# Two clips of the expert layer moved: two relus on ScalarE, and a product that subtracts on VectorE

## What is computed

```python
g = jnp.minimum(p1[..., 0::2], LIMIT)             # LIMIT = 7
lin = jnp.clip(p1[..., 1::2], -LIMIT, LIMIT)
act = g * jax.nn.sigmoid(ALPHA * g) * (lin + 1.0)
p2 = jnp.einsum('bsei,ehi->bseh', act, mlp2_weight) + mlp2_bias
combined = jnp.einsum('bseh,bse->bsh', p2, combine)   # combine: two weights of eight are not zero
```

## Time and profile before

| | |
|---|---|
| median of 3 runs | 915.94 us (915.14 to 916.11) |
| the profiled execution's own time | 917.65 us |
| its span, first to last instruction | 915.9 us |
| mean granted TensorE clock | 0.976 of full speed |
| busy: PE, DVE, ACT, POOL | 841.9, 712.3, 721.0, 484.2 us |

### The profile page before, as it was taken

One profiled execution on the slowest core, in us unless ns is written; L12 is line 12 of the kernel. 1 busy time (PEld: TensorE's weight loads), 2 busy tenths in 40 slices (PEclk: granted clock), 3 DMA queues, 4 the chain that ended last, 5 costly groups with the idle time before them and its releaser, 6 DMA issues.

```text
span 915.9 us, 37757 instructions
## 1 busy us (share of the span) xinstructions
PE 841.9 (92%) x15768; PEld 547.1 (60%) x15768; DVE 712.3 (78%) x1785; ACT 721.0 (79%) x1251; POOL 484.2 (53%) x786
## 2 busy tenths in 40 slices
PE   4569999999999999999999999999999999998996
PEld 2335666657566665756666575666657566665645
DVE  7666868879787887978788797878879787786635
ACT  4337888888788888888788888888888888877785
POOL 6417446382735638283653827366382736445352
PEclk9758999999999999999999999999999999999999
DMA  5952417133351613334261323416133341610101
GB/s 127 227 88 84 75 43 142 56 104 44 119 80 56 142 55 103 44 125 75 66 130 56 104 43 123 76 61 136 55 100 47 113 76 50 135 44 7 31 2 36
DMA packets 85597, 75.14 MB, mean 82 GB/s; under 512 B 9457, under 2 KB 79154, under 8 KB 85426
## 3 DMA queue, kind: packets, MB, share of 16 engines
q1 hardware_dynamic: 83346, 71.93, 34.9%
q10 hardware_dynamic: 2080, 0.79, 0.4%
HBM read 36.26 MB, written 30.15 MB: 73 GB/s over the span
## 4 chain that ended last, share of the span: by engine, by line
PE 64%; DVE 14%; issue 10%; ACT 7%; POOL 2%; DMA 2%; SPq 1%; POOLq 0%; DVEq 0%; ACTq 0%
PE ps L571 11%; PE ps L513 8%; PE ps L843 6%; PE ps L805 6%; PE ps L502 5%; PE ps L794 3%; PE ps L590 2%; DVE mx L1221 2%; PE ps L528 2%; PE ps L811 2%; PE ps L585 2%; ACT h L1077 2%; PE ps L719 2%; PE ps L781 2%; DVE act_t L1368 2%
## 5 line engine op out<-in xcount | busy, mean ns | idle before, releaser
L1221 DVE TENSOR_REDUCE mx<-ps 128x2 f32<-128x320 f32 (+1 forms) x512 | 219.7, 466 | 101.9 <-PE ps L528 100.8
L1004 ACT ACTIVATE pt<-ps 128x1024 f32<-128x1024 f32 (+1 forms) x256 | 232.9, 914 | 39.5 <-PE ps L502 37.2
L1487 POOL TENSOR_SCALAR_AFFINE_SELECT pt<-pt 128x512 f32<-128x512 f32 x256 | 162.3, 637 | 140.5 <-ACT pt L1004 139.5
L513 PE MATMUL ps<-kd,qz 48*32 48x160 bf16 (+1 forms) x4096 | 146.1, 236 | 13.8 <-issue 6.7
L502 PE MATMUL ps<-qz,kd 51*32 51x256 bf16 (+1 forms) x4096 | 153.6, 261 | 0.8 <-issue 0.7
L794 PEld LDWEIGHTS ps<-m,act_t 128*128 128x128 f32 x1024 | 128.1, 191 | 39.6 <-DVE act_t L1368 23.6
L571 PE MATMUL ps<-pt,va 128*32 128x256 f32 (+1 forms) x2048 | 145.2, 364 | 2.1 <-POOL pt L1490 0.9
L794 PE MATMUL ps<-m,act_t 128*128 128x128 f32 x1024 | 140.0, 280 | 7.6 <-DVE act_t L1368 5.7
L513 PEld LDWEIGHTS ps<-kd,qz 48*32 48x32 bf16 x4096 | 77.9, 92 | 105.9 <-issue 52.3
L1490 POOL TENSOR_SCALAR_AFFINE_SELECT pt<-pt 128x512 f32<-128x512 f32 x192 | 122.1, 636 | 0.0
L1037 ACT ACTIVATE lin<-ps,mbias 128x512 f32<-128x512 f32 x128 | 87.5, 684 | 35.5 <-DVE act_t L1368 22.9
(11 more groups left out here) (187 smaller groups left out, 1560.1 us busy)
## 6 DMA issues: line engine op xcount, KB each, us to landing
qz<-qk_parts SPq DMA_DIRECT2D x32, 384.0 KB, 6.4
kd<-qk_parts SPq DMA_DIRECT2D x32, 384.0 KB, 10.0
qk_parts<-qp SPq DMA_DIRECT2D x16, 384.0 KB, 3.1
qk_parts<-kp SPq DMA_DIRECT2D x16, 384.0 KB, 2.8
xl<-L_attn_x SPq DMA_DIRECT2D x16, 256.0 KB, 3.5
qk_parts<-qp SPq DMA_DIRECT2D x16, 256.0 KB, 3.1
qk_parts<-kp SPq DMA_DIRECT2D x16, 256.0 KB, 2.9
xnr<-xn SPq DMA_DIRECT2D x16, 256.0 KB, 2.5
```

What stands on the lines that cost most here:

```text
L513: nc.tensor.matmul(ps[QG * c:QG * (c + 1), 4 + par, w * pr:w * (pr + 1)], qz[q][rows, 2 * g + pr, P * i + QG * c:P * i + QG * (c + 1)], kd ...
L1004: nc.scalar.activation(to, src, ACT.Exp, scale=SCALE).then_inc(exp_ok.sem, 1)
L1221: nc.vector.tensor_reduce(mx[:, i, HG * g + pr:HG * (g + 1):2], src, AX.X, ALU.max).then_inc(mx_ok.sem, 1)
L1487: sel1 = nc.gpsimd.affine_select(out=pt[:, s, :, 0:P], in_=pt[:, s, :, 0:P], compare_op=ALU.is_ge, fill=0.0, base=0, pattern=[[0, HG], [1, ...
```

## The change

For the experts 4 and 6 (`TWICE`) the clip is made by two relus on ScalarE. The first takes the place of the plain eviction, with a bias of b + 1 + (LIMIT - 1), and gives max(p1, -7) + 7. The second (`clip_high`) reads and writes `lin` in SBUF, with a scale of -1 and a bias of 2 LIMIT, and gives 7 minus the clipped value; it stands right behind `evict_gate(e)` in ACT's list. VectorE has no clip for these two, and their product subtracts 1 + LIMIT from `lin` before it multiplies, which gives the product with its sign turned. The mask `sel` holds -1 in place of 1 for them, so that `gc` is negative too. For this the masks are made in 24 instructions (8 experts, 3 parts) in place of 3.

```diff
+TWICE = (4, 6)
+SIGNS = tuple((e, -1.0 if e in TWICE else 1.0) for e in range(8))
...
+        span = sb("span", [P, 1])
...
-            (half[:], -0.5), (ident[:], 0.0), ...
+            (half[:], -0.5), (span[:], 2.0 * LIMIT), (ident[:], 0.0), ...
...
                 def evict_lin(e):
                     act.wait_ge(*done(up_ps, b, e + 1))
                     act.wait_ge(*(done(act_ok, b, e - 1) if e >= 2 else done(act_ok, b - 1)))
-                    nc.scalar.activation(lin[:, e % 2], bank(3 * (e % 2) + 1), ACT.Identity, bias=mbias[:, e, 1:2]).then_inc(lin_ok.sem, 1)
+                    if e in TWICE:
+                        nc.scalar.activation(lin[:, e % 2], bank(3 * (e % 2) + 1), ACT.Relu, bias=mbias[:, e, 1:2]).then_inc(low_ok.sem, 1)
+                    else:
+                        nc.scalar.activation(lin[:, e % 2], bank(3 * (e % 2) + 1), ACT.Identity, bias=mbias[:, e, 1:2]).then_inc(lin_ok.sem, 1)
+
+                def clip_high(e):
+                    act.wait_ge(*done(low_ok, b, TWICE.index(e) + 1))
+                    nc.scalar.activation(lin[:, e % 2], lin[:, e % 2], ACT.Relu, scale=-1.0, bias=span[:]).then_inc(lin_ok.sem, 1)
...
                             evict_gate(e)
+                            if e in TWICE:
+                                clip_high(e)
...
+                dve.wait_ge(consts.sem, 3)
+                for e in TWICE:
+                    nc.vector.tensor_scalar(mbias[:, e, 1:2], mb_b[:, e, 1:2], 1.0, LIMIT - 1.0, ALU.add, ALU.add).then_inc(consts.sem, 1)
...
                 def clip(e):
 
+                    if e in TWICE:
+                        return
...
-                        dve.wait_ge(*done(clip_ok, b, e + 1))
-                        nc.vector.tensor_tensor(act_t[:, e % 3], lin[:, e % 2], gc[:, e % 2], ALU.mult).then_inc(act_ok.sem, 1)
+                        if e in TWICE:
+                            dve.wait_ge(*done(lin_ok, b, e + 1))
+                            nc.vector.scalar_tensor_tensor(out=act_t[:, e % 3], in0=lin[:, e % 2], scalar=1.0 + LIMIT, in1=gc[:, e % 2],
+                                                           op0=ALU.subtract, op1=ALU.mult).then_inc(act_ok.sem, 1)
+                        else:
+                            dve.wait_ge(*done(clip_ok, b, e + 1 - sum(t < e for t in TWICE)))
+                            nc.vector.tensor_tensor(act_t[:, e % 3], lin[:, e % 2], gc[:, e % 2], ALU.mult).then_inc(act_ok.sem, 1)
...
-                        pool.wait_ge(masks_set.sem, 7 + c)
-                    nc.gpsimd.affine_select(out=sel[:], in_=sel[:], compare_op=ALU.not_equal, fill=1.0, base=-E * c, pattern=[[-1, E], [0, P]],
-                                            channel_multiplier=1).then_inc(masks_set.sem, 1)
+                        pool.wait_ge(masks_set.sem, 7 + E * c)
+                    for e, sign in SIGNS:
+                        nc.gpsimd.affine_select(out=sel[:, e], in_=sel[:, e], compare_op=ALU.not_equal, fill=sign, base=-E * c - e, pattern=[[0, P]],
+                                                channel_multiplier=1).then_inc(masks_set.sem, 1)
```

More of the change, by code:

```diff
@@ L60 @@
 TIE = -1e-37
-CONSTS = 4
+CONSTS = 6
 AT_STATES, AT_H0, AT_Q, AT_K, AT_U, AT_V, AT_G, AT_C = 2, 3, 4, 6, 8, 10, 12, 14
@@ L309, in build @@
         lin_ok = signal("lin_ok", E)
-        clip_ok = signal("clip_ok", E)
+        low_ok = signal("low_ok", len(TWICE))
+        clip_ok = signal("clip_ok", E - len(TWICE))
         gc_ok = signal("gc_ok", E)
@@ L371, in build @@
         BLANKS = [
-            (half[:], -0.5), (ident[:], 0.0), (identb[:], 0.0), (bw[:, N:], 0.0), (cw[N:, :], 0.0), (ncw[:], 0.0), (b2st[:], 0.0),
+            (half[:], -0.5), (span[:], 2.0 * LIMIT), (ident[:], 0.0), (identb[:], 0.0), (bw[:, N:], 0.0), (cw[N:, :], 0.0), (ncw[:], 0.0), (b2st[:], 0.0),
             (edge[:], 0.0), (first[:], 0.0), (tie[:], 0.0), (sel[:], 0.0), (bias3[:], 0.0), (onesb[:], 1.0),
@@ L383, in build @@
         ALL_BLANKS = len(BLANKS) + len(LATER_BLANKS)
-        N_MASKS = 7 + NPART
+        N_MASKS = 7 + NPART * E
         qk_d = nc.dram_tensor("qk_parts", (2, P, 6, T), BF16, kind="Internal").ap()
```

## The result

The changed kernel takes 927.35 us (median of 4 runs, 925.24 to 927.63) against 915.92 (4 runs, 915.14 to 916.11): a ratio of 1.0109, 95% interval 1.0092 to 1.0126. The medians lie 11.4 us apart, the ratio gives 10.0 us (8.4 to 11.5). It is slower, as forecast, and inside the range, near its upper end; forecast were 8.4 us more, at 924.4. The profiled execution took 927.32 us, where 926.1 had been forecast for it.

The account below looks back on a forecast made before the run. ACT's full list was taken to hold h2T, for which PE's MLP waits. 15 x 0.55 + 0.18 = 8.4 us took the profiled 917.65 to 926.1, the median to 924.4; range 921.0 to 928.0.

Parts of the forecast that it names:

- Second relu of expert 4: On ACT between ga 4 and lin 5: hidden in the idle time before lin 5, with 0.2 us to spare.
- Second relu of expert 6: On ACT between ga 6 and lin 7, no idle time: delays h2T by 0.55 us a pass, ends 0.48 and 0.67.
- Pass 0: lin 7 there follows 0.26 us of idle time, so the delay is 0.18 us, with ends at 0.11 and 0.30.
- What waits behind h2T: PE's MLP follows 0.55 us later, its wait grows from 0.47 to 1.0 us; no second stall, nothing given back.
- First relu: On ACT in place of an Identity eviction from PSUM of the same tile: zero difference, at the dearest 0.10 us more.
- Clips of 4 and 6: Removed from DVE: product 4 comes 0.36 us earlier, product 6 does not move; gain on the path 0 for both.
- The product with a subtraction: On DVE, in place of the plain product of 0.69 us: no difference taken.
- Prologue: 24 mask selects on POOL take at most 7.0 us, covered by its wait for DVE: cost 0, without cover 3.4 once.
- A hidden delay: Rival: PE waits for something else behind L805 for at least 0.45 us a pass, time stays near 916; chance 0.08.
- A part given back in the attention stage: Case in which part of the delay is given back in the attention stage; chance 0.03.
- Relief of DVE: Rival: one clip of 0.36 us comes off each pass, 5.8 us in all, giving 910.1; chance 0.07.
- Table loads: Rival: relu needs another ACT table, 1.28 us a load, 61 us and 8.4, some 985; chance 0.02.

Follow-up runs that it names:

- The relu that nobody reads: Kernel before, all clips on VectorE, plus an unread relu behind ga 6 on ACT: 930.07 us against 916.26, the second time 927.35 against 916.45.
- the swap: h2T put ahead of lin 7 in ACT's list: 909.69 us against 916.45 in the kernel before; with relus for experts 2 and 3, 898.75.
- Expert 4 alone: The change made for expert 4 only, against the kernel before: 917.72 us against 917.32, ratio 1.0009.

## Why the prediction was right, point by point

- *h2T is held by ACT's own list, and a pass has no slack behind it.* Right. The relu that nobody reads delays `h2T` and the kernel with it; the swap makes both faster.
- *Second relu of expert 4: hidden.* Right. It starts 0.57 after ga 4, as worked out. Between its start and that of lin 5 are 0.77 us, of which it needs 0.61 to 0.62: 0.15 to spare, not 0.2, as the same price was set too low. Expert 4 alone costs nothing that can be measured.
- *Second relu of expert 6: on the path.* Right in place, too small in size. This is the mis-sized term: 0.55 us a pass was taken, 0.62 measured. I had placed it under the eviction of 0.69 us for its SBUF source; it takes 0.72, more than that eviction. The overlap with the next instruction was taken at 0.12 and is 0.11. Over 15 passes this made the forecast 1.0 us too low.
- *Pass 0.* `h2T` 12.86 us after `aoT` before and 13.08 after: 0.22 for 0.18.
- *What waits behind h2T.* Right that nothing gives the delay back: the shortest stretch to the next `aoT` is 40.50 us for 40.52. PE's wait was to be 1.0 us and is 1.22: product 5 comes 0.34 us earlier too, which had been left out, and lets down 5 end 0.13 earlier. That lengthens the wait and moves nothing.
- *First relu at no difference.* Right: L1042 takes 0.67 to 0.69, the eviction of before 0.67 to 0.70.
- *Clips of 4 and 6: no gain.* Right, the clip of 4 moves the products 4 and 5 by some 0.35 us and `h2T` not at all; product 6 stays in place, and so do the products of experts 2 and 3, whose moving was named as a sign of being wrong.
- *The product with a subtraction: no difference.* Right, 0.69, but for the one of pass 0.
- *Prologue: 0.* The masks took 6.34 us, within the bound of 7.0, and alone cost nothing measurable. The wait by which they are covered is 7.27 us.
- *The sum.* With the measured price it is 15 x 0.615 + 0.22 = 9.4 us, which the split of the span shows (9.40). The ratio gave 10.0 us at first and 10.4 us in a second comparison (927.43 against 916.26, ratio 1.0114, 1.0093 to 1.0135), the medians 11.4 and 11.2:

> The changed kernel once more, against the kernel before on one chip in five rounds. The stretch from the first aoT to h2T grew by 0.61 us in each of 15 passes and by 0.22 in pass 0: if nothing else is in the difference, the median ratio gives 9.4 us (9 to 10); if the prologue or another part costs as well, 11 us or more, as the first runs gave (11.4).

Both intervals hold 9.4 us (8.4 to 11.5, and 8.5 to 12.4). What the 0.6 to 2 us beyond 9.4 are is not settled. The profiled executions do not show them: 927.32 is 9.67 over 917.65, and outside `aoT` to `h2T` their spans come to 716.1 us before and to 716.2 and 716.0 changed. They may be chance: the median of the kernel before moved between 915.92, 917.32, 916.26 and 916.45 from set to set, and the kernel with the dead relu by 2.7 us. The part of the span outside `aoT` to `h2T` differs by 3 us between the two executions of the dead relu. That the change lengthens PE's pauses was neither shown nor shut out.

The forecast of 924.4 also took over that the profiled execution of before lay 1.71 us above its median. That of the changed kernel lies at its median. So of the 3.0 us between 924.4 and 927.35 the relu's price makes 1.0, and most of the rest is where the profiled executions happened to lie. The range was wide enough for both.

- *The rivals.* A hidden delay: no, PE shows no other wait. A part given back in the attention stage: no, by the shortest stretch. Relief of DVE: not at 4 and 6, but true at 2 and 3, ahead of product 3, where it is worth 0.34 us a clip. Table loads: none were added, 49 in both profiles. By the Trainium skill, "ScalarE: Activation LUTs", section Table sets, relu is in every set; the trace now agrees for Relu beside the sigmoid form of gelu. The rule of that page of the Trainium skill, section Rules for kernel authors, to keep relu, max and min off ScalarE gives as its reason the speed of VectorE in bf16, while this tile is f32. It held for the placement made here, and not for experts 2 and 3, where 0.72 us of an idle ACT buy 0.34 us of a full DVE.

## What to carry to other kernels

ScalarE was busy for 79% here and had its pauses at certain places: moving work to it was free in a pause and cost full price two experts later, so choose the instructions to move by what stands before the crossing on the giving engine and by the idle rows on the taking one. Price an added instruction by the distance from start to next start, and bound an unseen form from above by the dearest neighbour: this one came out above the form that it seemed nearest to, and inside the bound. And look at what an engine's list puts ahead of the instruction that another engine waits for: here a swap of two lines was worth 6.9 us.

## What had not been expected of the hardware

- A relu from SBUF to SBUF in f32, 128 x 512, with an immediate scale and a bias column, takes 0.72 us (up to 0.74 for experts 2 and 3), more than the 0.69 of an eviction from PSUM with a bias column, and is no cheaper when it isn't in place (0.72).
- In one kernel the expert stages repeat to 0.02 us from pass 1 on, but PE pauses in the attention stages for up to 1.2 us with no semaphore to wait for. The pauses come back at the same places of PE's list in different executions and kernels, and 17 of 21 follow a packet on the instruction queue by 1.4 to 1.8 us. They are a part of the 3 us by which two profiled executions of one kernel differ here.
